# Decoder of twelve stages: in the last stage, GpSimd's inverse root of the heads' norms as a maximum and a power

## The reference, cut to what matters

```python
def l2norm(t):
    return t / jnp.maximum(jnp.linalg.norm(t, axis=-1, keepdims=True), 1e-12)
...
def attn_layer(x, Wqkv, qs, ksc, Wo):
    b, n, _ = x.shape
    qkv = x @ Wqkv
    q, k, v = jnp.split(qkv, 3, -1)
    ...
    q = l2norm(q) * qs
    k = l2norm(k) * ksc
    ...
    q = q * cos * scale + rotate_half(q) * sin * scale
    inv = 1.0 / scale
    k = k * cos * inv + rotate_half(k) * sin * inv
    out = local_attention(q, k, v)
    ...
for i in range(DEPTH):
    x = attn_layer(shift_tokens(x), Wqkv[i], q_scale[i], k_scale[i], Wo[i]) + x
    x = ffn_layer(shift_tokens(x), ln_g[i], ln_b[i], W1[i], b1[i], W2[i], b2[i]) + x
```

## Time and profile before

| what | value |
|---|---|
| median of 3 runs | 2918.16 us (2910.07 to 2920.03) |
| span of the profiled execution | 2892.0 us; the runs' times also hold what lies around the span, 26.2 us at the median |
| last stage | from about 1785 us to the end of the span |
| PE busy over the span | 2565.0 us (89%) |
| DVE, ACT, POOL busy | 1798.9 us (62%), 1537.1 us (53%), 1365.0 us (47%) |

### The profile page before, as it was taken

The page is one execution under the profiler, slowest core; times in us unless marked ns, Lnnn a source line. Parts: engine busy times, 40 slices in busy tenths (PEclk is TensorE's granted clock), DMA queues, the critical chain, the costliest instruction groups (busy, mean ns, idle before and its releaser), DMA issues. The chain is left out here.

```text
span 2892.0 us, 56780 instructions
## 1 busy us (share of the span) xinstructions
PE 2565.0 (89%) x20009; PEld 1646.1 (57%) x20009; DVE 1798.9 (62%) x4074; ACT 1537.1 (53%) x4979; POOL 1365.0 (47%) x1981
## 2 busy tenths in 40 slices
PE   6999978898989979866589997899999999999997
PEld 3555545555646646544345554566666666666665
DVE  4566655545657745555555555777677777777773
ACT  1455535524747736532245553566665666666654
POOL 0344434302536614300024444876776777767762
PEclk8899988999989999988799998999999999999998
DMA  2000000010000010000100001010101101011000
GB/s 69 1 1 1 1 8 2 12 33 5 2 4 2 2 33 1 6 1 8 28 1 1 1 1 58 12 38 20 31 23 31 34 20 30 27 27 34 20 25 7
DMA packets 45707, 47.77 MB, mean 17 GB/s; under 512 B 11947, under 2 KB 31414, under 8 KB 45431
## 3 DMA queue, kind: packets, MB, share of 16 engines
q1 hardware_dynamic: 45430, 44.18, 5.5%
HBM read 31.05 MB, written 0.52 MB: 11 GB/s over the span
## 5 line engine op out<-in xcount | busy, mean ns | idle before, releaser
L2264 ACT ACTIVATE net_probs<-bank,net_negmax 128x96 f32<-128x96 f32 x768 | 250.9, 338 | 191.4 <-DVE net_negmax L2397 191.2
L1033 DVE TENSOR_REDUCE negmax<-scores 128x1 f32<-128x508 f32 (+4 forms) x512 | 212.5, 467 | 211.2 <-PE scores L918 180.0
L1013 POOL TENSOR_TENSOR l_xattn_probs<-l_xattn_probs,rowinv 128x512 f32<-128x512 f32 x128 | 130.3, 1039 | 406.5 <-DVE rowinv L1025 406.5
L2326 POOL TENSOR_TENSOR net_probs<-net_probs,net_inverse 128x384 f32<-128x384 f32 x192 | 158.7, 826 | 237.8 <-DVE net_inverse L2393 237.8
L1013 POOL TENSOR_TENSOR lora_probs<-lora_probs,rowinv 128x508 f32<-128x508 f32 (+1 forms) x256 | 149.5, 617 | 246.2 <-DVE rowinv L1025 246.2
L2397 DVE TENSOR_REDUCE net_negmax<-bank 128x4 f32<-128x384 f32 x192 | 106.3, 554 | 242.9 <-PE bank L2099 242.3
L2318 POOL TENSOR_TENSOR net_rope<-net_rope,net_sin_parts 128x512 f32<-128x512 f32 x192 | 243.8, 1270 | 5.5 <-DVE net_sin_parts L2367 5.4
L124 DVE COPY turned<-flip 128x512 f32<-128x512 f32 (+3 forms) x280 | 163.0, 582 | 65.8 <-PE flip L945 52.9
L2336 POOL TENSOR_TENSOR net_rope<-net_rope,net_head_inv 128x512 f32<-128x512 f32 x192 | 201.2, 1048 | 0.0
L739 DVE TENSOR_REDUCE negmax<-scores 128x2 f32<-128x256 f32 (+2 forms) x192 | 157.6, 822 | 63.2 <-PE scores L647 35.5
L918 PE MATMUL scores<-kT,qM 64*128 64x512 f32 (+2 forms) x768 | 188.2, 567 | 8.3 <-ACT kT L122 4.8
(11 more groups left out here) (434 smaller groups left out, 6546.3 us busy)
## 6 DMA issues: line engine op xcount, KB each, us to landing
net_w_qkv<-in_L_ffn_Wqkv SPq DMA_DIRECT2D x12, 768.0 KB, 5.7
net_vals_between<-net_vals SPq DMA_DIRECT2D x48, 192.0 KB, 2.5
net_w_out<-in_L_ffn_Wo SPq DMA_DIRECT2D x6, 512.0 KB, 4.2
net_vals_between<-net_vals SPq DMA_DIRECT2D x48, 64.0 KB, 2.0
moe_w<-in_L_ffn_w13T SPq DMA_DIRECT2D x8, 256.0 KB, 2.7
net_w<-in_L_ffn_W SPq DMA_DIRECT2D x6, 341.0 KB
moe_w<-in_L_ffn_w2T SPq DMA_DIRECT2D x8, 128.0 KB, 2.4
ctx_tok<-in_ctx SPq DMA_DIRECT2D x1, 768.0 KB, 6.5
```

What stands on the lines that cost most here:

```text
L1013: last = nc.gpsimd.tensor_tensor(own, own, rowinv[:, u * tail + w:u * tail + w + 1].to_broadcast([P, k1 - k0]), ALU.mult)
L1033: last = nc.vector.tensor_reduce(negmax[:, u * tail + w:u * tail + w + 1], scores[:, 2 * qt + h, k0:k1], AX.X, ALU.max, negate=True)
L2264: last = nc.scalar.activation(prob_blocks(g)[:, w, :], score_blocks(g)[:, w, :], ACT.Exp, bias=maxima[:, g % 4, w:w + 1], accum_out=sums[: ...
L2326: nc.gpsimd.tensor_tensor(prob_blocks(g), prob_blocks(g), part, ALU.mult).then_inc(shared.sem, 1)
```

## The change

`inverse_root` becomes a maximum into `net_head_temp` and one `tensor_tensor` with the operation `pow`, whose second operand is a tile that holds -0.5 (`net_head_power`, filled once by DVE at the start of the stage). `ROOT_OPS` goes from 14 to 2, and with it the counts that POOL (L2333) and DVE (L2431) wait for. `root_of_variance` on DVE stays as it is.

```diff
-                head_temp = sbl("head_temp", [P, 3, QT * 2 * HB])
+                head_power, head_temp = sbl("head_power", [P, QT * 2 * HB]), sbl("head_temp", [P, QT * 2 * HB])
...
-                made = signal("window_made", 4)
+                made = signal("window_made", 5)
...
+                        nc.vector.memset(head_power[:, :], -0.5).then_inc(made.sem, 1)
...
-        ROOT_OPS, ROOT_MAGIC = 14, float(0x5F3759DF - (1 << 30) - (1 << 22))
+        ROOT_OPS, ROOT_MAGIC = 2, float(0x5F3759DF - (1 << 30) - (1 << 22))
...
-            half, y, t = temp[:, 0, :], temp[:, 1, :], temp[:, 2, :]
-            done = [before]
-            def then(ins, last=False):
-                done[0] += 1
-                ins.then_inc(step.sem, 1)
-                if not last:
-                    pool.wait_ge(step.sem, step.at(0, done[0]))
-            then(nc.gpsimd.tensor_scalar(half, src, floor, -0.5, ALU.max, ALU.mult))
-            then(nc.gpsimd.tensor_scalar(y.bitcast(I32), half.bitcast(I32), -0.5, ROOT_MAGIC, ALU.mult, ALU.add))
-            for r in range(3):
-                then(nc.gpsimd.tensor_tensor(t, y, y, ALU.mult))
-                then(nc.gpsimd.tensor_tensor(t, t, half, ALU.mult))
-                then(nc.gpsimd.tensor_scalar(t, t, 1.5, None, ALU.add))
-                then(nc.gpsimd.tensor_tensor(y if r < 2 else out, t, y, ALU.mult), last=(r == 2))
-            assert done[0] - before == ROOT_OPS
+            nc.gpsimd.tensor_scalar(temp, src, floor, None, ALU.max).then_inc(step.sem, 1)
+            pool.wait_ge(step.sem, step.at(0, before + 1))
+            nc.gpsimd.tensor_tensor(out, temp, power, ALU.pow).then_inc(step.sem, 1)
...
-                            inverse_root(pool, head_sums[:, j % 2, :], 1e-24, head_inv[:, j % 2, :], head_temp, rooted, ROOT_OPS * j)
+                            inverse_root(pool, head_sums[:, j % 2, :], 1e-24, head_inv[:, j % 2, :], head_power[:, :], head_temp[:, :], rooted, ROOT_OPS * j)
```

More of the change, by code:

```diff
@@ L1851, in l3_ffn, with inverse_root @@
                 stream(p, GT, qkv_in, (rope, sin_parts, squares, vals, mid), (w_qkv, w_out, w1, w2, vec), (qk_rows, sines, cosines, sin_table, cos_table),
-                       (head_sums, head_inv, head_temp), (ln_inv, ln_shift, ln_temp), (qk_T, probs, flat_p, maxima, sums, inverse, window16),
+                       (head_sums, head_inv, head_power, head_temp), (ln_inv, ln_shift, ln_temp), (qk_T, probs, flat_p, maxima, sums, inverse, window16),
                        (late, znT, gelu, acts))
         by_batch = lambda v: v.rearrange("p (b n) -> p b n", b=B)
-        ROOT_OPS, ROOT_MAGIC = 14, float(0x5F3759DF - (1 << 30) - (1 << 22))
-        def inverse_root(pool, src, floor, out, temp, step, before):
-            half, y, t = temp[:, 0, :], temp[:, 1, :], temp[:, 2, :]
-            done = [before]
-            def then(ins, last=False):
-                done[0] += 1
-                ins.then_inc(step.sem, 1)
-                if not last:
-                    pool.wait_ge(step.sem, step.at(0, done[0]))
-            then(nc.gpsimd.tensor_scalar(half, src, floor, -0.5, ALU.max, ALU.mult))
-            then(nc.gpsimd.tensor_scalar(y.bitcast(I32), half.bitcast(I32), -0.5, ROOT_MAGIC, ALU.mult, ALU.add))
-            for r in range(3):
-                then(nc.gpsimd.tensor_tensor(t, y, y, ALU.mult))
-                then(nc.gpsimd.tensor_tensor(t, t, half, ALU.mult))
-                then(nc.gpsimd.tensor_scalar(t, t, 1.5, None, ALU.add))
-                then(nc.gpsimd.tensor_tensor(y if r < 2 else out, t, y, ALU.mult), last=(r == 2))
-            assert done[0] - before == ROOT_OPS
+        ROOT_OPS, ROOT_MAGIC = 2, float(0x5F3759DF - (1 << 30) - (1 << 22))
+        def inverse_root(pool, src, floor, out, power, temp, step, before):
+            nc.gpsimd.tensor_scalar(temp, src, floor, None, ALU.max).then_inc(step.sem, 1)
+            pool.wait_ge(step.sem, step.at(0, before + 1))
+            nc.gpsimd.tensor_tensor(out, temp, power, ALU.pow).then_inc(step.sem, 1)
         def stream(p, GT, qkv_in, rows, weights, tables, heads_norm, ln, softmax, ffn):
@@ L1901, in stream @@
             qk_rows, sines, cosines, sin_table, cos_table = tables
-            head_sums, head_inv, head_temp = heads_norm
+            head_sums, head_inv, head_power, head_temp = heads_norm
             ln_inv, ln_shift, ln_temp = ln
```

## The result

The changed kernel takes **2923.61 us** (median of 20 runs, 2916.07 to 2931.01) against 2914.09 (20 runs, 2897.22 to 2924.44): a ratio of 1.003, 95% interval 1.0018 to 1.0043. The forecast was 2891 us, faster with a chance of 0.53; the time lies in the range (2884 to 2986), on the other side of before, 9.5 us slower and just outside the 8.8 us that the forecast counted as no change. The changed kernel's runs fall in two groups of ten, 2916 to 2920 and 2927 to 2931 us (group medians 5 and 14 above before's), and none lies near their common median.

The account below looks back on a forecast made before the run. PE was busiest, with DVE's norm chain, held by POOL's add, on its path once a job. Held time -23.3, filling -4 and setup +0.1 summed to -27.2 us, giving 2891 us; range 2884 to 2986.

Parts of the forecast that it names:

- The price of the power … I take 2.2: POOL's root, last stage: one power of 128x32 estimated at 2.2 us from 30 passes, with ends 0.25 and 7.0.
- POOL is out of the way if … p under 2.8. All 23.3 us go: Steady jobs: with a power under 2.8 us, POOL's add ends before DVE's norm chain can be held, saving 23.3 us.
- the norm chain is on the path one to one: DVE's layer-norm Newton chain, once a job ahead of the next maximum: a job's length follows the chain's one to one.
- Above 3.1 DVE is held for p - 3.1, by L2318 or by the power itself: DVE's norm chain: a power of p us above 3.1 holds it for p - 3.1, against 1.06 us before.
- rival 1: Last stage: a long power makes DVE wait, slower from 4.16 us; at 6 us 47.5 us more, 2966 us; chance 0.29.
- The filling … I take 4: Start of the last stage, PE's four waits for its scaling behind POOL's first roots: 4 us less, from nothing to 6.4.
- 26.2 us for what lies around it: Distance of the median 2918.16 us from the profiled span 2892.0, kept when turning the forecast span into a time.
- The page's chain of waits: Profile page: it gives POOL 25% of the span; the forecast said not to follow it, since POOL waits for DVE.
- Rivals 3 and 4: Last stage: POOL becomes full from a 9.4 us power (0.06); other POOL work takes the add's place (no own chance).

Follow-up runs that it names:

- one round: The kernel before with one round of Newton refinement in the root instead of three (six operations, coarser): 2878.40 against 2920.57 us, 0.9859.
- probe: The changed kernel with a block ahead of the last stage timing POOL powers and multiplies of several widths beside small DVE operations; power of 128x128 20.786 us.
- the add-first kernel: The changed kernel with POOL's add of the rotary parts issued ahead of the root instead of behind it: 2895.36 against 2920.57 us, 0.9904.
- the one with Newton first: Newton's fourteen operations for the first 6 of 48 roots, the power for the other 42: 2917.46 against 2920.57 us for the kernel before, 0.9988.
- the one with the power first: The power for the first 6 of 48 roots, Newton's fourteen operations for the other 42: 2922.22 against 2909.93 us for the kernel before, 1.0042.

## Why the prediction failed

The forecast failed at two steps, the price p of the power and the rule for what DVE loses when p is long. They err in opposite directions. With p as measured the forecast's own rule gives 2918 + 33 = 2951 us; that the time lies within its range comes from the range's width and not from the rule.

- **"The price of the power … I take 2.2": wrong, the first failed step.** It is 5.46, inside the ends 0.25 and 7.0. No run shows the 30 passes that the 2.2 was made of. The argument that a step inside one instruction costs less than a pass has no support in the runs: each element costs 160 ns where a multiply's costs 2.2. By the pass of the forecast (0.068 us for 32 elements) the power is worth (5.46 - 0.18) / 0.068 = 78 passes. The figure of the Trainium skill's "GPSIMD Engine Reference" (3.1 Elementwise — side-by-side cycle accounting), 2.6 cycles an element, does not hold for the power. The Trainium skill's "Trainium Architecture — The Big Picture" (The software stack), which warns of surprisingly slow opcodes on POOL, was the better guide: the 5.46 us agree with the warning. That a software handler is the reason was not shown.
- **"POOL is out of the way if … p under 2.8. All 23.3 us go": right as a rule, not met.** With a short root (one round) the jobs gain 933.9 - 909.0 = 24.9 us and the filling 9.5. That the norm chain is on the path one to one stands: 1.06 us less chain in each of 21 jobs is 22.3, and the two long jobs that vanish are 3.2 more, 25.5 together against 24.9. The forecast missed that last part, the 3.8 us at the end, and in the filling the clock: of the 9.5 us there 2.9 are PE's busy time (65.70 to 62.82) at a granted clock of 1.00 instead of 0.95.
- **"Above 3.1 DVE is held for p - 3.1, by L2318 or by the power itself": wrong, the second failed step.** A power of 128x32 holds DVE for 0.3 us at its start, one of 128x128 for 0.5 (probe), and neither afterwards (the add-first kernel). In the changed kernel only the add holds the chain, for one stretch of some 1.0 us wherever it falls in it. So the held time did not grow with p, and rival 1's mechanism in the jobs did not come about: no chain is longer than 3.30, some 0.96 above the free 2.33, where the rule asked for 2.36. Of rival 1 only the filling's part has a counterpart in the runs. By the same rows a power some 0.9 us longer would put the add (now at 2311.33) behind the chain's free end (2309.91 + 2.33) and let the chain go free, as in the kernel with the add first; that is an estimate, and no run tried it. The Trainium skill's "SBUF — State Buffer" (Who interferes with whom) says of a shared-port conflict that the first has the pair "for the whole instruction". In these runs that holds for the add and the 128x512 multiply, and not for the power.
- **"The filling … I take 4" less: wrong sign, from p.** With 5.80 us from a root's start to the add's (2305.53 to 2311.33) instead of 4.66, four waits should grow by 4 x 1.14 = 4.6; they grew by 4.4. The term has a second half that I left out: longer waits brought a lower clock, 3.8 us.
- **"26.2 us for what lies around it": wrong reading, harmless to the sum.** The forecast was made as a difference from the median, and that stands. The distance was that one execution's early part, which was quicker; what lies around a span is 2 us.
- **The page's chain of waits is misleading: right.** It names POOL for 25 to 27% of the span in both kernels, and forty-two powers in the jobs cost nothing that can be seen. Rivals 3 and 4 didn't come about.

## What to carry to other kernels

Before an operation replaces a handful of cheap ones, measure it at two widths on the engine: the power costs by the element, a multiply hardly does, so fourteen small operations (4.66 us) beat a maximum and a power (5.80). When one engine's chain is held by a long operation of another, look first at where that operation stands in its queue: issuing one add ahead of the root was worth 29 us (25 by the split), while the exchange of the arithmetic moved the time by 9 (5). Read the start of a pipelined stage by itself, since an engine with slack in the steady part can be the bound there.

## What the runs showed of the hardware that was not expected

**A long GpSimd operation need not hold VectorE.** Of the 102 small DVE operations that lie wholly under the 20.8 us power, 101 took 0.16 to 0.17 us. The one held ended 0.49 us after the power's start, and the 128x128 multiply takes 0.46; at 128x32 the two are 0.27 and 0.25. A reading that fits is that POOL first fetches its operands and then computes without the ports; what it does inside was not measured. A 128x512 multiply or add holds DVE to its end, a `tensor_scalar` with one input (1.12 us in the probe) just as a `tensor_tensor` (1.13 and 1.19 in the kernels). In the probe no `tensor_tensor` was caught by a multiply of 128x512: six of seven started 0.02 us ahead of one, the seventh behind the last, and all took 0.16.

**Two jobs of 21 lose the clock after PE's wait.** In the kernel before, the changed one and the one with Newton first, two jobs are 1.4 to 1.8 us longer than the rest (three in the one with the power first), with a granted clock of 0.96 instead of 1.00. In the five kernels where PE waits 1.1 to 1.3 us a job in place of 2.1 to 2.2, there is none. PE in such a job of the changed kernel, behind its wait (the same matmul takes 1.12 in other jobs):

```profile
2359.97 2.07 PE L2068 MATMUL bank<-net_w_qkv,xnT 128*128 128x512 f32 x2 [2.08 <-ACT net_rope L122]
2361.84 0.52 PE L2076 MATMUL bank<-net_window,ident 128*128 128x384 bf16 x1
2362.30 1.25 PE L2081 MATMUL bank<-net_qk_T 64*64 64x64 f32 x16
2363.48 0.66 PE L2093 MATMUL bank<-ident,net_rope 128*128 128x128 f32 x4
```

The first three take 1.5 us more than the 1.12, 0.33 and 0.83 of an ordinary job in the kernel before, and the fourth is back at 0.66. The window of these three:

```profile
2359.80:2363.20 3.40, 3.23 (x15) 1.55 (x17) 2.29 (x4) 1.72 (x5) 1.83 (x3) 0.50 0.00 0
```

Of the two levels of the clock, 1.2 and 2.4 GHz, that is the lower one for some 3 us after a wait (a mean of 0.96 over 45.75 us is 3.7 us at half speed). Why two of 21 equal waits and not all was not settled. It is not scatter alone: in the changed kernel they are the eleventh and the twenty-first job, and in the probe's kernel, which runs the same stage behind another block, the same two (45.78 and 45.75 us).
